# Moving half of the shared expert behind the routed expert blocks, with four smaller reorderings

## What is computed

```python
x = x + L0_attention(layernorm(x), ctx, mask)          # one head of width 256
x = x + L0_experts(layernorm(x))                       # 16 dense experts + 1 shared expert
x = x + L1_attention(layernorm(x), ctx, mask)          # 16 heads of width 16, then an output layernorm

def L1_experts(x):                                     # of layernorm(x)
    logits = flat @ router_w.T
    scores = softmax(logits)
    topk_idx = top_k(logits + router_bias, 2)
    # weights of the two chosen experts, divided by their sum
    for e in range(16):
        h = silu(flat @ Wu[e]) * (flat @ Wg[e])
        out += combine[:, e] * (h @ Wd[e])
    out += (silu(flat @ Su[0]) * (flat @ Sg[0])) @ Sd[0]   # the shared expert, hidden width 256
    return out
x = x + L1_experts(layernorm(x))
```

## Time and profile before

| | us |
|---|---|
| median of 3 runs | 773.53 (770.79 to 775.27) |
| the profiled execution | 771.28 |
| its span in the trace | 769.4 |
| TensorE busy in it | 698.4 |
| VectorE busy | 536.7 |
| ScalarE busy | 395.6 |
| GpSimd busy | 175.4 |
| mean granted clock of TensorE | 0.981 |

### The profile page before, as it was taken

The page is one execution under the profiler, slowest core; times in us unless marked ns, Lnnn a source line. Parts: engine busy times, 40 slices in busy tenths (PEclk is TensorE's granted clock), DMA queues, the critical chain, the costliest instruction groups (busy, mean ns, idle before and its releaser), DMA issues.

```text
span 769.4 us, 14908 instructions
## 1 busy us (share of the span) xinstructions
PE 698.4 (91%) x5499; PEld 526.6 (68%) x5499; DVE 536.7 (70%) x1174; ACT 395.6 (51%) x564; POOL 175.4 (23%) x220
## 2 busy tenths in 40 slices
PE   4789989899899999999999798899999999998990
PEld 3678878798677888888888554455455455576880
DVE  6656566557576666666667788579888888875655
ACT  2633323234232222222222599799999999633550
POOL 5460624521001000000000050002302702632561
PEclk9999999999999999999999999999999999999995
DMA  7355474652535766776678939886997860274545
GB/s 244 131 167 209 144 251 157 211 203 86 177 85 172 252 225 214 255 245 209 221 256 162 189 65 203 142 114 98 202 135 168 118 98 2 93 305 112 165 138 191
DMA packets 55212, 131.16 MB, mean 170 GB/s; under 512 B 12160, under 2 KB 29952, under 8 KB 51568
## 3 DMA queue, kind: packets, MB, share of 16 engines
q1 hardware_dynamic: 51888, 122.93, 60.1%
q0 software_dynamic: 2256, 6.18, 2.2%
q10 hardware_dynamic: 1008, 1.25, 0.5%
HBM read 78.78 MB, written 48.79 MB: 166 GB/s over the span
## 4 chain that ended last, share of the span: by engine, by line
PE 50%; ACT 11%; DVE 11%; DMA 10%; issue 9%; POOL 6%; SPq 2%; DVEq 0%; POOLq 0%; ACTq 0%
PE ps L653 12%; PE ps L654 11%; PE ps L655 11%; ACT p L1433 7%; PE ps L996 5%; PE ps L1184 3%; PE ps L954 3%; DMA raw<-in_ctxT 2%; DMA qst<-ql 2%; DMA raw<-in_ctxN 2%; POOL cTl L609 2%; DMA k_lo<-kl 2%; PE ps L1200 2%; POOL cNl L596 1%; ACT cNh L1263 1%
## 5 line engine op out<-in xcount | busy, mean ns | idle before, releaser
L1433 ACT ACTIVATE p<-ps,kbias 128x1024 f32<-128x1024 f32 (+1 forms) x208 | 211.1, 1153 | 9.8 <-PE ps L954 9.8
L1937 DVE TENSOR_SCALAR p<-p 128x1024 f32<-128x1024 f32 (+1 forms) x208 | 140.5, 688 | 29.5 <-ACT p L1433 27.9
L996 PE MATMUL ps<-p,vsl 128*17 128x256 f32 (+1 forms) x1664 | 115.2, 385 | 1.4 <-DVE p L1937 1.3
L954 PEld LDWEIGHTS ps<-qst,kst 48*128 48x128 f32 (+1 forms) x832 | 58.7, 182 | 63.7 <-ACT p L1433 32.0
L1339 ACT ACTIVATE hh<-h 128x512 fp32r<-128x512 f32 x50 | 31.6, 632 | 132.4 <-DVE h L1808 115.4
L954 PE MATMUL ps<-qst,kst 48*128 48x256 f32 (+1 forms) x832 | 90.8, 318 | 9.3 <-DMA qst<-ql 4.2
L359 POOL TENSOR_SCALAR nv<-mv 128x2 f32<-128x2 f32 x8 | 6.2, 778 | 360.4 <-DVE mv L1871 209.9
L653 PE MATMUL ps<-xTh,w_hi 128*128 128x512 f32 x200 | 79.8, 399 | 1.5 <-DVE h L1804 0.8
L654 PE MATMUL ps<-xTl,w_hi 128*128 128x512 f32 x200 | 79.2, 396 | 0.0
L655 PE MATMUL ps<-xTh,w_lo 128*128 128x512 f32 x200 | 78.9, 394 | 0.0
L996 PEld LDWEIGHTS ps<-p,vsl 128*17 128x17 f32 (+1 forms) x1664 | 35.7, 97 | 40.4 <-DVE p L1937 8.3
(11 more groups left out here) (308 smaller groups left out, 1550.2 us busy)
## 6 DMA issues: line engine op xcount, KB each, us to landing
x_slots<-blank SPq DMA_DIRECT2D x20, 1032.0 KB, 5.9
kst<-k_hi SPq DMA_DIRECT2D x64, 200.2 KB, 9.0
w_raw<-in_w SPq DMA_DIRECT2D x25, 384.0 KB, 3.6
v_one<-vst SPq DMA_DIRECT2D x4, 1768.0 KB, 8.6
vsl<-v_one SPq DMA_DIRECT2D x4, 1768.0 KB, 15.8
kst<-k_lo SPq DMA_DIRECT2D x32, 200.2 KB, 8.4
raw<-in_ctxN SPq DMA_DIRECT2D x12, 512.0 KB, 5.3
k_hi<-kh SPq DMA_DIRECT2D x24, 256.0 KB, 2.6
```

Source lines behind the costliest of these rows:

```text
L954: mm = pe.matmul(ps[0:rows, 2 * (x % RING) + t, c * SEQ:(c + 1) * SEQ], kst[r, job % KSL, c, m * P:m * P + rows], qst[r, b, 2 * g + c, :], ...
L996: mm = pe.matmul(ps[32 * j:32 * j + VW, 6 + job % 2, 0:SEQ], vsl[0:rows, b % 2, at_:at_ + VW], p32[0:rows, x % PBUF, (2 * t + c) * SEQ:(2 ...
L1433: act.activation(p32[0:rows, x % PBUF, :], psf[0:rows, bank * 512:bank * 512 + 1024], ACT.Exp, scale=0.25, bias=kbias[0:rows, col:col + 1] ...
L1937: dve.tensor_scalar(t, t, CLO, CHI, ALU.max, ALU.min).then_inc(p_clip, 1)
```

## The change

Five edits, together:

1. **Shared expert, second 512 tokens.** `gates(1, ...)`, `ups(1, ...)`, `shared_down(1, ...)` go from in front of the expert blocks to behind them on PE, and with them their Silus, products and splits on ACT and DVE. Their sums are added to the residual rows between the two halves of the mix.
2. **Early ranks.** With the products gone, `ranks` of the last two tiles follows the last logits directly on PE.
3. **Early row numbers.** SP waits for `eb_rdy` first, loads the row numbers of the first four blocks, and only then waits for the scatters (`slots_out`). In later blocks the load stands ahead of the waits.
4. **First pair alone.** DVE finishes tiles 0 and 1 up to their normalisation before it sums tiles 2 and 3. The second pair's transpose comes behind the first queries; the queries of sequence pair 0 come at steps 0 and 3 instead of before the loop and at step 1.
5. **Values later.** `values(1)` is issued behind `keys(4)` instead of between `keys(3)` and `queries(0, 3)`.

```diff
                 keys(job)
                 if job == KSL:
+                    queries(0, NG - 1)
+                if job == KSL + 1:
                     values(1)
-                    queries(0, NG - 1)
...
-            sp.wait_ge(slots_out, 16 * 2 * NT)
-
-            sp.wait_ge(eb_rdy, 2)
...
+            first_rows = [row_of(j) for j in range(XR)]
+            sp.wait_ge(slots_out, 16 * 2 * NT)
             for j in range(XR):
-                slots_in(j)
+                slots_in(j, first_rows[j])
...
-            for q in range(2):
-                pair_T(q, q)
+            pair_T(0, 0)
...
-            pe.wait_ge(ln_lo, 6)
-            queries(0, 7)
+            pair_T(1, 6)
 
             def early(y):
-                if y == 1:
+                if y == 0:
+                    pe.wait_ge(ln_lo, 6)
+                    queries(0, 7)
+                elif y == 3:
                     queries(1, 6)
...
-            pe.wait_ge(silu_rdy, SC0 + 1)
-            gates(1, 0, 4)
-            pe.wait_ge(mul1_rdy, SC0 + 1)
-            ups(1, 0, 5)
-            pe.wait_ge(silu_rdy, SC0 + 2)
-            gates(1, 1, 6)
             pe.wait_ge(pre_ev, NB - 1)
             ranks(NB, NT - 2, NT, ps[:, 1, :])
...
-            pe.wait_ge(mul1_rdy, SC0 + 2)
-            ups(1, 1, 0)
...
-            pe.wait_ge(hl_rdy, SC0 + 4)
-            shared_down(1, 6)
...
                     expert_down(j - 1)
+            gates(1, 0, 0)
+            ups(1, 0, 1)
+            gates(1, 1, 2)
+            ups(1, 1, 3)
+            pe.wait_ge(hl_rdy, SC0 + 4)
+            shared_down(1, 4)
...
                     hidden_ev(j)
+            shared_silu(2, 0)
+            shared_silu(3, 2)
+            shared_high(2)
+            shared_high(3)
             act.wait_ge(pos_rdy, NB + 1)
...
-            for q in range(2):
-                tiles_add(q)
-                tiles_mean(q, 1)
...
+            tiles_add(0)
+            tiles_mean(0, 1)
+            pair_norm(0)
+            tiles_add(1)
+            tiles_mean(1, 1)
+            pair_lo(0, 0)
+            pair_norm(1)
...
+            shared_mul(2, 1)
+            shared_mul(3, 3)
+            shared_low(2)
+            shared_low(3)
             dve.wait_ge(s_exp, 1)
...
-            dve.wait_ge(add_rdy, 8)
             for t in range(NT):
+                if t == NT // 2:
+                    shared_add(2, 4)
+                    shared_add(3, 5)
```

More of the change, by code:

```diff
@@ L543, in _, with row_of, slots_in @@
                 sp.dma_start(e_w[:, NSH1 + 8 * n:NSH1 + 8 * n + 8, :], a["w1"][NSH1 + 8 * n:NSH1 + 8 * n + 8].rearrange("k p c -> p k c")).then_inc(d_in[1], 16)
[L544 to L553 removed]
+            sp.wait_ge(eb_rdy, 2)
+            def row_of(j):
+                return sp.value_load(rb_i[0:1, j:j + 1], min_val=0, max_val=NFILL * CAP - P)
+            def slots_in(j, row):
+                sp.dma_start(xb[:, j % XR, :], xs_d[bass.ds(row, P), :]).then_inc(xb_in[j % XR], 16)
+            first_rows = [row_of(j) for j in range(XR)]
+            sp.wait_ge(slots_out, 16 * 2 * NT)
             for j in range(XR):
[L556 removed]
+                slots_in(j, first_rows[j])
             for j in range(XR, NBLK):
[L558 removed]
+                row = row_of(j)
+                sp.wait_ge(xT_rdy, j - XR + 1)
+                sp.wait_ge(yi_rdy, j - XR + 1)
+                slots_in(j, row)
             for n in range(4):
@@ L1461, in _ @@
             shared_high(0)
-            shared_silu(2, 4)
             shared_high(1)
-            shared_silu(3, 6)
-            shared_high(2)
-            shared_high(3)
             def slots_ev(j):
@@ L1892, in queries_lo, with pair_norm @@
                                          op0=ALU.add, op1=ALU.subtract).then_inc(q_lo, 1)
-            for q in range(2):
-                tiles_add(q)
-                tiles_mean(q, 1)
-            for q in range(2):
+            def pair_norm(q):
                 dve.wait_ge(ln_std, 5 + q)
@@ L1902, in _ @@
                 tile_norm(2 * q + 1)
-            for q in range(2):
-                pair_lo(q, q)
+            tiles_add(0)
[5 more added lines that the diff above has]
+            pair_norm(1)
             tiles_add(2)
@@ L1908, in _ @@
             tiles_add(3)
+            pair_lo(1, 6)
             def early(x):
-                if x == 0:
+                if x == 1:
                     queries_lo(0, 3, 7)
-                elif x == 1:
+                elif x == 3:
                     queries_lo(1, 4, 6)
-                elif x == 4:
+                elif x == 5:
                     tiles_mean(2, 2)
@@ L2213, in _ @@
             dve.tensor_scalar(past_e[:, NBLK:2 * NBLK], past_e[:, 0:NBLK], room_e, None, ALU.mult).then_inc(sel_rdy, 1)
-            shared_mul(2, 5)
-            shared_mul(3, 0)
-            shared_low(2)
             dve.wait_ge(pre_rdy, NB + 3)
@@ L2220, in _, with shared_add @@
             link(dve.tensor_scalar(eb_r[:], ps[:, 7, 256:256 + NBLK], -1.0, float(E), ALU.mult, ALU.add))
-            shared_low(3)
             link(dve.tensor_reduce(m_top[:], m_l[:], AX.X, ALU.max))
             dve.tensor_tensor(m_e[:], m_l[:], spread(m_top), ALU.subtract).then_inc(pos_rdy, 1)
-            for q in range(4):
+            def shared_add(q, bank):
                 x = resid[:, 2 * q:2 * q + 2, :].rearrange("p t d -> p (t d)")
                 dve.wait_ge(down_done, SC0 + q // 2 + 1)
-                dve.tensor_tensor(x, x, ps[:, (2, 3, 6, 7)[q], :], ALU.add).then_inc(add_rdy, 1)
+                dve.tensor_tensor(x, x, ps[:, bank, :], ALU.add).then_inc(add_rdy, 1)
+            for q in range(2):
+                shared_add(q, 2 + q)
             def hidden_mul(j):
```

21 lines of the change are left out of this document (8 added, 13 removed).

## The result

The changed kernel takes **774.68 us** (median of 14 runs) against **769.27 us** of the kernel before (median of 14 runs): ratio 1.0072, 95% interval 1.0045 to 1.0098. One of the 14 runs of the changed kernel took 3672.7 us; it is in the median but not in the ratio, and the median of the other 13 is 774.36 us. So it is slower, by some 5.5 us (3.5 to 7.5). The range of the prediction, 769.4 to 777.4, holds the time. The forecast was 773.7, but for a change of +1.0 us: it stood on a level of 772.7 us for the kernel before, 3.4 above the level that the comparison found. The change itself was therefore forecast 4.5 us too small, and its sign beyond 0.5% ("slower", 0.18) was not the likely case of the prediction.

A forecast was written before the change was run, and what follows sets the result against it. PE carries half the chain, with ACT's Exps pacing the second attention; -4.2 - 0.45 + 1.3 + 4.3 = +0.95 us, say +1.0, on a mean of 772.7 gives 773.7 us, range 769.4 to 777.4.

The forecast's parts named there:

- slower: Whole kernel: slower than before by over 0.5%, given a chance of 0.18.
- Edit 5 (-4.2): Second attention, step 39: PE's wait for the queries' transfer to `qst` goes wholly, -4.2 us.
- rival B: Second attention: the stall moves to late values at `pv(52)`; price up to 3.7 us, total +4.7, 777.4; chance 0.10.
- C: Second attention: queries still land late, half the stall stays, +2.1 us; total +3.1, 775.8; chance 0.12.
- Edit 4 (-0.45): Start of second attention: first Exp at most 1.2 us earlier, partly given back by large queries in the first steps, -0.45.
- In front of and in the blocks (+1.3): Expert blocks and before: earlier scatters and row numbers against half-clock products, +1.3 us, from -1.5 to +2.7.
- a spell of 3.3 us: PE in `shared_down(0)` and first blocks: clock at half for 3.3 us, costing +1.5 and +1.4 us.
- the upper end that the prediction named (+2.9): PE in front of the blocks: top of the 0 to 2.9 us range for `shared_down(0)` at half the clock.
- edit 3, put at -0.1: SP before the blocks: four early loads, paid with late row numbers, bring the second transfer only 0.1 us earlier.
- Behind the blocks (+4.3): Tail: mix starts 3.0 us later and holds two additions of 1.28 us; +4.3, from 3.8 to 4.8.
- A: In front of the blocks: PE's clock stays at 2.4 GHz, -1.5 instead of +1.3; total -1.85, 770.9; chance 0.22.
- D: Attention and blocks: later ACT waits shrink too and gaps stay warm; total -3.9, 768.8; chance 0.08.

The follow-up runs named there:

- the kernel with the moved work alone: Changed kernel with edits 4 and 5 undone, leaving the moved shared expert, early ranks and early row numbers: 777.41 us, ratio 1.0105 to the kernel before.
- the values alone: Kernel before with only values(1) issued behind keys(4): 767.07 us, ratio 0.9968 to the kernel before.
- The run with the two chains exchanged: Changed kernel with the router weights' Exp and eleven small operations ahead of the shared expert's second half: 771.92 us, ratio 1.0012 to the kernel before.
- the filled kernels: Changed kernel plus 39 unread products in PE's idle time: 771.17 us; the same with Exp and small operations ahead of the shared expert's second half: 766.78 us.
- the values and two row numbers: Kernel before with values(1) behind keys(4) and the first two row numbers loaded before the scatter wait: 765.22 us, ratio 0.9936.
- the same kernel with the handover's products: Kernel before with values later and two early row numbers, plus 14 unread products at the handover to the second attention: 765.82 us, ratio 0.9931.

## Why the prediction was right and wrong, point by point

**Edit 5 (-4.2): right in size, not in weight.** The stretch got 4.33 us shorter, and by itself 4.21. No wait for `vsl` came up: rival B did not happen, nor did C. But the prediction counted the stall of the earlier trace rows as fixed. It is a meeting of two chains, the queue of SP and the steps of ACT, and shrinks when the steps are late: the kernel with the moved work alone had 1.2 us of it. If such executions are common, the gain in the mean is less than 4.2; the ratio of the values alone, -2.5 us, points there, though its interval also holds -4.3. How often the stall is small was not measured.

**Edit 4 (-0.45): not refuted, and not measurable.** The mean of the executions gives -0.4, the timing 1.0001. The mechanism was as described: a lead of 1.8 us at the first Exp (the prediction had 1.2 at most), given back by the queries that stand in the first steps.

**In front of and in the blocks (+1.3): the term that was too small.** Measured +3.86, and it falls into five pieces, read between marks of both traces.

| us | predicted | before | after | difference |
|---|---|---|---|---|
| last Exp to ranks | -0.65 | 21.68 | 21.06 | -0.62 |
| ranks to `shared_down(0)` | 0 | 4.47 | 5.36 | +0.89 |
| `shared_down(0)` | +1.5 | 2.94 | 5.41 | +2.47 |
| `blocks_of_experts` to transposes of `xb` | -0.95 | 6.04 | 5.69 | -0.35 |
| transposes to L | +1.4 | 51.15 | 52.62 | +1.47 |

The first and the last were right: the ranks had waited only some 0.65 us for the removed products, and the start of the blocks at half the clock costs 1.47. But the 0.62 us never reached the scatters, whose last one landed no earlier after the last Exp than before (32.15 us against 32.02). Two terms were mis-sized by one reason. The clock was expected back after a spell of 3.3 us, 1.9 us into unbroken work, taken from the earlier trace rows. It stayed at 0.50 from about 678 to 690, over idle times of 3.44, 1.59 and 1.44 us and over 5 us of unbroken work in `shared_down(0)`; so all 24 products ran at half the clock, the upper end that the prediction named (+2.9), and the ranks and the small products did too, which it had at nothing. The small products lie on the chain: DVE waits for each. What made `shared_down(0)` weigh in full is its place: the row numbers stand behind it on PE. Before, that was hidden, since the scatters ended last (695.16); in the changed kernel nothing hides it. `blocks_of_experts` ahead of `shared_down(0)` would have had its inputs at 685.42, 5.1 us before it ran, and the scatters (690.86) would then have been last, an estimated 3 us before the first transfer as it was (694.07 less 690.86). No run tests this.

The third was edit 3, put at -0.1 in sum with the late row numbers. The sum made the two loads its measure, and let the early loads run from 693.9 against scatters at 694.5. In the trace the row numbers are written 1.9 us later than that relative to the attention's end (691.39 less 658.71, against 693.9 less 663.15), and all four loads then stand between them and the first transfer. The second transfer, which the prediction wanted some 5 us earlier than before, went at 694.65, only 2.7 us earlier than 697.37. The prediction's sentence "the early loads are paid with the late row numbers" was true; it did not ask what the changed kernel would do without them: with the loads in the old place it is some 1.0 us faster at L.

**Behind the blocks (+4.3): right, +4.30.** The mix starts 2.98 us later (predicted 3.0) and holds the two additions of 1.28. `shared_down(1)` fell to half the clock at about 759 and was ready before the mix reached its middle, as foreseen. The run with the two chains exchanged shows that 2.9 us of it were a matter of order. Behind the table load the Exp follows at once (757.15 plus 1.28, Exp at 758.44), as in the earlier trace rows; a further drain of 1.38 us, as the Trainium skill has it (ScalarE: Activation LUTs, What ACT_TABLE_LOAD costs), is not in this trace either, nor in the run where two loads stand in a row (at 750.56 and 752.18 for 1.28 each, their operations at 751.85 and 753.48).

**The rivals.** A, the full clock, was the right question with the wrong side for this kernel, and the filled kernels show what it is worth: 3.6 to 5.2 us, not the 2.8 between its -1.5 and the forecast's +1.3. B, C and D didn't occur.

**The level.** The time came out 1.0 us from the forecast because two errors nearly cancelled, the level of before taken too high by 3.4 and the change too small by 4.5. That is luck. Four executions are too few for a level: those of before lie between 764.6 and 777.5 us.

## What to carry to other kernels

Work that fills PE's waits is not free to move: when it goes, price the clock at half for all the work behind the gap, small products on the chain included, and for the first microseconds of the next unbroken stretch too (5 us here), and take the upper end if further idle times stand in between. Then look whether a short step on the chain stands behind long work in the program of its engine: what was hidden there before isn't any more. When loads are made early, ask for the later of their two inputs, since loads behind the late one are merely moved in front of the first transfer. Of two chains behind the last block, the one that a transfer covers goes first.

## What the runs showed of the hardware

- 39 products whose results nobody reads made a kernel faster: by 3.6 us in one execution's blocks, and the same 39 by 5.2 us in another, by whether the granted clock fell in `shared_down(0)`.
- The same instructions behind the same idle times find the clock at 1.00 in one execution and at 0.50 in another. Both filled kernels idle about 0.55 and then 1.49 us in front of `shared_down(0)`; one had the full clock there, the other 0.50 from 684 to 687. So it was with the values and two row numbers (3.0 us for `shared_down(0)`) and the same kernel with the handover's products (0.59 in 684 to 686), 1.49 us idle in both.
- The start of the last `down` products of the dense experts, behind 420 us of the same work, scattered over 6 us between executions, and the stretch from there to the 11th Exp over 3.3 us (23.47 to 26.77) in the five kernels whose program there is that of before. Differences of single traces are to be taken between near marks.
- A register load with its arithmetic took 0.54 to 0.57 us on SP in a row of four (starts at 691.41, 692.25, 692.82, 693.36), and 0.84 for the first.
